# A transformer block in float32: the projections in another order, every input loaded in place

## The reference

```python
ctx_img = context[:, :257]; ctx_txt = context[:, 257:]
q = rms_norm(linear(layernorm(x), q_w, q_b), norm_q_w)          # 16 heads of 32
k = rms_norm(linear(ctx_txt, k_w, k_b), norm_k_w);  v = linear(ctx_txt, v_w, v_b)
k_img = rms_norm(linear(ctx_img, k_img_w, k_img_b), norm_k_img_w);  v_img = linear(ctx_img, v_img_w, v_img_b)
x = x + linear(attention(q, k_img, v_img) + attention(q, k, v), o_w, o_b)
# then a chain of small layers on the last token of each batch, a gate over all tokens, and a layer norm
```

## Time and profile before

| | |
|---|---|
| median of 3 runs | 604.54 us (603.22 to 607.73) |
| profiled execution | 605.41 us, its span 603.6 us |
| busy: PE, DVE, ACT, POOL | 533.3, 401.6, 282.0, 238.8 us |
| mean clock of TensorE granted | 0.952 of full speed |
| moved by DMA | 91.92 MB, mean 152 GB/s |

### The profile page before, as it was taken

How to read it: one execution, slowest core, us unless ns; L and a number is a source line. 1 busy time by engine, 2 the same in 40 slices (tenths; PEclk the granted TensorE clock), 3 DMA queues, 4 the chain that set the end, 5 groups by cost and what they waited for, 6 DMA issues and landing times.

```text
span 603.6 us, 9876 instructions
## 1 busy us (share of the span) xinstructions
PE 533.3 (88%) x3800; PEld 326.2 (54%) x3800; DVE 401.6 (67%) x783; ACT 282.0 (47%) x504; POOL 238.8 (40%) x138
## 2 busy tenths in 40 slices
PE   2599889999989999999999987899998999999860
PEld 2477667987655655555555553444353545454320
DVE  4547886522987788568875786566556666448676
ACT  2355844553135556436664342636252444376352
POOL 0033230022025677427655352152433063667453
PEclk9988989999989999989999987899899999799986
DMA  9506677499589778935987471707071623100001
GB/s 286 185 2 243 219 265 282 165 205 313 198 196 311 207 196 193 235 115 131 236 231 200 124 168 72 171 0 171 1 171 71 136 70 110 71 1 36 18 35 52
DMA packets 56512, 91.92 MB, mean 152 GB/s; under 512 B 5553, under 2 KB 30257, under 8 KB 55953
## 3 DMA queue, kind: packets, MB, share of 16 engines
q1 hardware_dynamic: 52000, 75.26, 45.5%
q0 software_dynamic: 3184, 14.16, 6.7%
q10 hardware_dynamic: 1280, 1.88, 1.0%
HBM read 71.08 MB, written 19.40 MB: 150 GB/s over the span
## 4 chain that ended last, share of the span: by engine, by line
PE 70%; DVE 15%; ACT 5%; POOL 4%; issue 2%; DMA 1%; ACTq 0%; POOLq 0%; DVEq 0%
PE psum L667 13%; PE psum L761 12%; PE psum L724 11%; PE psum L742 10%; PE psum L766 6%; PE psum L798 5%; DVE negt L1149 4%; PE psum L887 3%; PE psum L852 3%; PE psum L833 2%; DMA lows<-lows 1%; POOL ssum L1327 1%; POOL ssum L1325 1%; DVE qst L1179 1%; POOL ssum L1326 1%
## 5 line engine op out<-in xcount | busy, mean ns | idle before, releaser
L995 ACT ACTIVATE prob<-psum 128x512 f32<-128x512 f32 x256 | 138.7, 594 | 178.1 <-PE psum L742 178.0
L1149 DVE TENSOR_REDUCE negt<-psum 128x1 f32<-128x255 f32 (+1 forms) x256 | 129.2, 546 | 0.0
L1375 POOL TENSOR_TENSOR added<-added,prob 128x1024 f32<-128x1024 f32 x48 | 113.6, 2367 | 20.7 <-ACT prob L995 16.2
L724 PE MATMUL psum<-kst,qst 96*128 96x512 f32 x256 | 99.6, 466 | 4.9 <-DVE negt L1149 4.8
L1372 POOL TENSOR_TENSOR added<-prob 128x1024 f32<-128x1024 f32 x16 | 38.2, 2385 | 160.3 <-ACT prob L995 160.3
L742 PE MATMUL psum<-qst,kst 112*128 112x256 f32 x512 | 93.6, 303 | 1.9 <-ACT prob L995 1.8
L742 PEld LDWEIGHTS psum<-qst,kst 112*128 112x128 f32 x512 | 80.4, 197 | 24.8 <-ACT prob L995 10.9
L1147 DVE TENSOR_REDUCE negt<-psum 128x1 f32<-128x257 f32 x128 | 53.6, 419 | 60.3 <-PE psum L724 58.8
L761 PE MATMUL psum<-prob,vring 128*32 128x256 f32 x1152 | 91.9, 402 | 0.0
L724 PEld LDWEIGHTS psum<-kst,qst 96*128 96x128 f32 x256 | 41.2, 194 | 65.9 <-issue 40.3
L1325 POOL TENSOR_TENSOR ssum<-sq 128x512 f32<-128x512 f32 x6 | 9.6, 1598 | 110.8 <-ACT sq L960 110.8
(11 more groups left out here) (152 smaller groups left out, 678.0 us busy)
## 6 DMA issues: line engine op xcount, KB each, us to landing
kst<-kscr SPq DMA_DIRECT2D x96, 256.0 KB, 6.1
vring<-vscr SPq DMA_DIRECT2D x16, 576.0 KB, 8.4
kscr<-hl SPq DMA_DIRECT2D x16, 512.0 KB, 2.8
d<-d POOLq DMA_DIRECT2D x8, 1024.0 KB, 6.0
qst<-qscr SPq DMA_DIRECT2D x96, 64.0 KB, 6.2
vscr<-vbuf SPq DMA_DIRECT2D x18, 256.0 KB, 3.0
raw<-ctxT SPq DMA_DIRECT2D x4, 1024.0 KB, 5.1
qscr<-hl SPq DMA_DIRECT2D x8, 512.0 KB, 3.8
```

Of the source, the lines that this page charges most:

```text
L724: pe.matmul(psum[:, n % 3, :], qst[0:96, slot, jj, qt * P:(qt + 1) * P], kst[0:96, slot, jj, half * 512:(half + 1) * 512], start=True, sto ...
L995: act.activation(prob[:, r % NP, part], score2[:, part], ACT.Exp).then_inc(exp2_done, 1)
L1149: dve.tensor_reduce(negt[:, u % 2, qt, half, HPG + j:HPG + j + 1], psum[:, n % 3, k0:512], AX.X, ALU.max, negate=True)\
L1375: pool.tensor_tensor(added[:, :], added[:, :], prob[:, r % NP, :], ALU.add).then_inc(added_done, 1)
```

## The change

- **Order.** The second key tile of batch 0 comes first, then the first key tile, V of batch 0, xT and queries of half 1, xT and queries of half 0, keys (1,0), keys (1,1), V of batch 1. `TILE_TOKENS` says which of the two token buffers a tile reads.
- **First tile in pieces.** Its context tile and `wk` are loaded in four pieces each, split piece by piece, and PE runs `k01(kc)`: for each 128 input channels the three products of all four output chunks, in four banks.
- **In place.** `raw` is gone. Each input lands in the place of its own low part, which DVE then writes over it. All but one are issued at the start, without waits; `c11` is issued from ACT's queue (`late_ctx`) when tile 3 has been projected. `wk` and the four constants go on ACT's queue, the small late constants on SP's.
- **Loads apart.** `load_k` and `load_q` of units 0 and 1 have places of their own in the list.
- **Around V of batch 1.** S1(0) to S1(3) stand between the jobs of keys (1,1), S1(4) to S1(11) one to a job of V; the last four norms follow V jobs 4 to 7, and `shift(0)` job 4.
- POOL's memset of `chx` waits for the last sum of squares too.

```diff
+    split = lambda name: add('split', SPLIT_OF[name])
+    for kc in range(KC):
+        add('split', 2 * kc)
+        add('split', 2 * kc + 1)
+        add('k01', kc)
+    add('consts')
+    split('c00')
+    split('wki')
+    proj(0)
+    proj(1, (0,))
+    split('wvi')
+    proj(1, (1,))
+    split('wv')
+    proj(1, (2,))
+    add('sumsq', 0)
+    proj(1, (3,))
     add('xstat', 1)
     add('xnorm', 1)
+
+    for c in range(4):
+        v(0, (c,))
+        add('norm', 0, c)
+        if c == 1:
+            split('wq')
+        if c == 2:
+            add('sumsq', 1)
+    v(0, (4,))
+    add('xstat', 0)
+    add('norm', 1, 0)
+    v(0, (5,))
     for n in range(4):
         add('xT', 1, n)
+    add('norm', 1, 1)
+    v(0, (6,))
     add('xnorm', 0)
+    add('norm', 1, 2)
+    v(0, (7,))
+    add('norm', 1, 3)
+
+    proj(2, (0, 1, 2))
     for n in range(4):
         add('xT', 0, n)
+    proj(2, (3,))
+    add('load_k', 0)
+    split('c10')
+
+    proj(3, (0, 1))
+    add('sumsq', 2)
+    add('norm', 2, 0)
+    add('load_q', 0)
+    proj(3, (2,))
+    add('norm', 2, 1)
+    proj(3, (3,))
+    add('late_ctx')
+    add('norm', 2, 2)
+    add('norm', 2, 3)
+    add('load_k', 1)
+    add('load_q', 1)
+
+    proj(4, (0, 1))
+    add('sumsq', 3)
+    split('c11')
+    add('norm', 3, 0)
+    proj(4, (2,))
+    add('norm', 3, 1)
+    proj(4, (3,))
+    add('norm', 3, 2)
+    add('norm', 3, 3)
+
+    for oc in range(KC):
+        proj(5, (oc,))
+        if oc == 2:
+            add('sumsq', 4)
+        add('S1', oc)
+    after = {0: (('load_v', 0), ('load_v', 1), ('norm', 4, 0)), 1: (('norm', 4, 1),), 2: (('sumsq', 5), ('norm', 4, 2), ('norm', 4, 3)),
+             3: (('maxes', 0),), 4: (('norm', 5, 0), ('shift', 0)), 5: (('norm', 5, 1),),
+             6: (('norm', 5, 2),), 7: (('norm', 5, 3),)}
+    for c in range(CH):
         v(1, (c,))
+        add('S1', KC + c)
+        for e in after[c]:
+            add(*e)
     add('load', 2)
     add('phase2')
...
+TILES = [('k', 0, 1), ('k', 0, 0), ('q', 1), ('q', 0), ('k', 1, 0), ('k', 1, 1)]
+TILE_TOKENS = (0, 1, 1, 0, 1, 0)
+
+PIECES = [(n, kc) for kc in range(KC) for n in ('c01', 'wk')]
+SPLITS = [n for n, kc in PIECES] + ['c00', 'wki', 'wvi', 'wv', 'wq', 'c10', 'c11']
...
+            for kc in range(KC):
+                sp.dma_start(c_in['c01'][:, kc, :], ctx_of('c01')[:, kc, :]).then_inc(piece_loaded[2 * kc], 16)
+            load_c('c00')
+            load_w('wki')
+            load_w('wvi')
+            load_w('wv')
             load_x(1)
+            load_w('wq')
             load_x(0)
+            load_c('c10')
...
+            def load_q(u):
+                h, b, g = unit(u)
+                if u == 0:
+                    sp.wait_ge(lo_done, SPLIT_OF['c10'] + 1)
+                if u < 2:
+                    n = KC * TILES.index(('q', h)) + g
+                    for s in range(2):
+                        sp.wait_ge(hl_stored[s], 16 * ((n - s) // 2 + 1))
...
+            def k01(kc):
+
+                pe.wait_ge(lo_done, 2 * kc + 2)
+                for oc in range(KC):
+                    job = job_at[('proj', 0, oc, 0)]
+                    for a, b in ((0, 0), (0, 1), (1, 0)):
+                        mm = pe.matmul(psum[:, bank_of[job], :], w_parts['wk'][:, a, kc, oc * P:(oc + 1) * P],
+                                       token_parts[0][:, b, kc, :], start=(kc == 0 and a + b == 0), stop=(kc == KC - 1 and a == 1))
+                    if kc == KC - 1:
+                        mm.then_inc(job_done, 1)
...
+            for kc in range(KC):
+                act.dma_start(w_in['wk'][:, kc, :], T['wk'][kc * P:(kc + 1) * P, :]).then_inc(piece_loaded[2 * kc + 1], 16)
             for dst, src in ((ident[:, :], T['ident']), (colp[:], T['cols']), (ind_in[:, :], T['ind']), (lows[:, :], T['lows'])):
                 act.dma_start(dst, src).then_inc(const_loaded, 16)
 
-            def consts():
...
+            def late_ctx():
+                act.wait_ge(job_done, last_q[0] + 1)
+                act.dma_start(c_in['c11'][:], ctx_of('c11')).then_inc(in_loaded['c11'], 16)
```

More of the change, by code:

```diff
@@ L103, in make_plan @@
[L103 to L149, removed]
-        v(1, (c,))
[L151 to L160, removed]
@@ L268, in make_plan @@
     return plan
[L272 to L274 removed]
+TILES = [('k', 0, 1), ('k', 0, 0), ('q', 1), ('q', 0), ('k', 1, 0), ('k', 1, 1)]
+TILE_TOKENS = (0, 1, 1, 0, 1, 0)
+PIECES = [(n, kc) for kc in range(KC) for n in ('c01', 'wk')]
+SPLITS = [n for n, kc in PIECES] + ['c00', 'wki', 'wvi', 'wv', 'wq', 'c10', 'c11']
+SPLIT_OF = {n: i for i, n in enumerate(SPLITS)}
 JOBS = {'xT': 'dve', 'proj': 'act', 'sumsq': 'act', 'v': 'act', 'vimg': 'act', 'shift': 'dve', 'o': 'dve',
@@ L507, in last_job, with split_parts, ctx_of @@
             return max(n for n, e in enumerate(jobs) if test(e))
[L510 to L516, removed]
+        last_q = [last_job(lambda e: e[0] == 'proj' and e[1] == 3 - h) for h in range(2)]
+        def split_parts(i):
+            name = SPLITS[i]
+            if i < len(PIECES):
+                kc = PIECES[i][1]
+                if name == 'wk':
+                    return w_in['wk'][:, kc, :], w_parts['wk'][:, 0, kc, :], w_parts['wk'][:, 1, kc, :], piece_loaded[i]
+                return c_in['c01'][:, kc, :], token_parts[0][:, 0, kc, :], token_parts[0][:, 1, kc, :], piece_loaded[i]
+            if name[0] == 'w':
+                return w_in[name][:], w_parts[name][:, 0], w_parts[name][:, 1], in_loaded[name]
+            dst = token_parts[0 if name[2] == '1' else 1]
+            return c_in[name][:], dst[:, 0], dst[:, 1], in_loaded[name]
         last_k = last_job(lambda e: e[0] == 'proj')
+        def ctx_of(name):
+            c0 = int(name[1]) * KEYS + int(name[2]) * 512
+            return T['ctxT'].rearrange("(k p) n -> p k n", p=P)[:, :, c0:c0 + 512]
         block = ctx.enter_context(nc.Block())
@@ L593, in load @@
                         sp.dma_start(qst[row:row + 32, slot].bitcast(F32), src).then_inc(pair_loaded[slot], 16)
+            def load(u):
+                load_k(u)
+                load_q(u)
             def phase2():
@@ L631, in f_out @@
                   .then_inc(out_stored, 16)
-            steps = {'split': split, 'norm': norm, 'vstore': vstore, 'load': load, 'load_v': load_v, 'phase2': phase2,
+            steps = {'norm': norm, 'vstore': vstore, 'load_k': load_k, 'load_q': load_q, 'load': load, 'load_v': load_v, 'phase2': phase2,
                      'ch_row': ch_row, 'f_out': f_out}
@@ L928, in split @@
             def split(i):
[L929 to L934, removed]
+                src, hi, _, loaded = split_parts(i)
+                act.wait_ge(loaded, 16)
+                if SPLITS[i] == 'c10':
+                    act.wait_ge(job_done, last_q[1] + 1)
+                act.activation(hi, src, ACT.Copy).then_inc(hi_done, 1)
             def xstat(h):
```

105 lines of the change are left out of this document (46 added, 59 removed).

## The result

| | before | changed |
|---|---|---|
| median of 20 runs | 605.86 us (602.78 to 612.45) | 612.19 us (607.20 to 616.51) |
| profiled execution, its span | 605.41, 603.6 us | 613.36, 611.6 us |
| mean granted clock | 0.952 | 0.936 |

The ratio is 1.0098, with a 95% interval of 1.0075 to 1.0121. The change makes the kernel 1% slower. I had forecast 598, 1% faster.

The account below looks back on a forecast made before the run. PE has no gap from 200 us, so attention's start decides. S1(16) at 174.2 against 182.24 gains 8.0, less 1.3 for the clock: 6.7. 605.41 - 6.7 = 598.7, against the median 597.8, so 598; range 588 to 607.

Parts of the forecast that it names:

- Start and k01: First tile: eight ACT transfers issued by about 5.2 us, PE starts k01(0) at 8.3, its 48 matmuls end at 21.2.
- The constants: Wait before the second tile: constants land at 17 us, then DVE work until 22.6, a PE wait of 1.4.
- the third rival: Constants arrive late: ACT's queue slow, they land at 28 us, second tile at 32.6, 10 us lost, 608 us; chance 0.12.
- The dense stage: From the second tile PE runs dense through k(0,0), V, transposes and queries, ending at 78.2 us.
- T: The end of PE's dense stage, after q(1) and xT(0), forecast at 78.2 us.
- The stores that hold up DVE: After T: key loads delay query stores, DVE reduces S1(0) only after T + 40.6; PE waits 6.8 us, S1(3) ends at 129.4.
- The last norm and load(2): Around V of batch 1: norm(5,3) ends at 163.2, S1(16) follows 11.0 later at 174.2, PE waiting some 4 us.
- load(2) lands a first pair in about 8.2: Before S1(16): half a unit of issue, 4.1 us, and 4.6 for a transfer to land, less what overlaps.
- The restart: After the wait at S1(16) PE restarts at a low clock, worth 1.3 us of work.
- Everything after it is the same code in the same order: Premise of the sum: from S1(16), at 182.24 us before, nothing changes, so the gain there is kept.
- The rivals: Nobody is held up, 589 us (chance 0.22); the saving is handed back, 603 (0.18); constants arrive late, 608 (0.12).
- Handed back: Rival: before attention the store takes 10.1 us, POOL and DVE slow each other, 5 us later, 603 us; chance 0.18.

Follow-up runs that it names:

- a_pairs: The changed kernel with loads of units 2 and up again issued pair by pair, keys then queries of each pair: 595.93 us, ratio 0.9842 to the kernel before.
- a_late8: The changed kernel, keys first, with POOL's 1 MB weight loads two steps earlier in units 1 to 7 only: 603.21 us, ratio 0.9958 to the kernel before.

## Why the prediction was wrong, by its own steps

**Start and k01.** 8.3 forecast, 8.91 measured. The eight issues on ACT ended at 5.60 instead of 5.2. The 48 matmuls took 13.62 instead of 12.9 and ended at 22.53 instead of 21.2.

**The constants, and the third rival.** They were in at 15.95, DVE's first use of them, against my 17, and the second tile starts at 22.55 against 22.6, with no gap on PE (its first weight load waited 0.44). That the time fits is luck: the constants did not set it. DVE's subtraction for wki began at 20.20, behind ACT's copies, which waited for c00 until 15.78 and for wki until 18.25; by my rate those first 4 MB should have been in at 16.4. Had k01 ended at 21.2 as forecast, PE would have stood for 1.3 us, for wki and not for the constants. The rival that had ACT's queue starve until 28 is refuted: a megabyte of key pieces and the constants got through within 16 us. (That rival's second tile, 32.6, left out the 1 us of work on the constants: 33.6.) The Trainium skill (DMA: Bandwidth & Descriptors, Queues, rings and completion order) has each DMA engine take turns between its queues, from which the prediction made an estimate of 15. The measured 15.95 lies much nearer to it than to the 28 by ind_in's pace; but the prediction doesn't show how it came to 15, so this supports the rule only loosely.

**The dense stage.** T was to be 78.2; q(1)'s last job ends at 72.69 + 2.75 = 75.4. The mis-sized term is the transposes. I took the 3.2 us that 16 of them took before; by tile the changed kernel has

```profile
L705 PE MATMUL psum<-ident,xin x32: 270/272/273, 55.3 to 72.7; 128*128 128x128 f32 x32
```

and takes 1.7 for 16. Before they came after a gap, partly at half clock: the granted clock was 0.74 from 29 to 31 us and 0.50 from 31 to 33. Two times 1.5 us.

**The stores that hold up DVE.** DVE starts on S1(0) 42 us after T, at 117.34; the sum had 40.6. The wait for POOL was 1.77 (1.6) and for c11 1.57 (1.5). But the step gave PE's wait as one of 6.8 us for DVE. It was 3.03 for ACT at S1(0), whose second bank still held proj(5,0), then half clock (0.50 from 110 to 116), and 1.35 for DVE at S1(1). ACT in turn had waited for POOL to add up tile 4's squares:

```profile
107.65 1.59 POOL L1380 TENSOR_TENSOR ssum<-ssum,sq 128x512 f32<-128x512 f32 x1
...
109.27 0.69 ACT L1013 ACTIVATE raw<-psum,colp 128x512 f32<-128x512 f32 x1 [4.50 <-POOL ssum L1380]
```

The forecast has no such wait. So the time was nearly right and its split was not, which again is partly luck. S1(3) ends at 125.9 against 129.4, most of that from T.

**The last norm and load(2).** norm(5,3) was stored at 160.15 against 163.2. Up to here the forecast was 3 us too careful, about what T was off. (The 33.8 in it is also added up wrongly: eight tiles at 1.26, eight norms at 1.85, 1.8 and 6 make 32.7; it took 34.2.) Then it failed, in the term "load(2) lands a first pair in about 8.2". I had split a unit's issue into halves from a timeline in which pairs go in order, and hadn't read `load` in the diff for the order of its transfers. I had counted the transfers that stand ahead of others on SP's queue for units 0 and 1 only. Measured from the store to S1(16): 16.3 us instead of 11.0, a wait of 7.67 instead of 4. With the pairs in order it is 172.85 - 161.35 = 11.5 (a_pairs), so the term was right for the old order.

**The restart.** 1.3 us in the sum. From S1(16) to unit 0's end it took 10.3 before and 14.0 now, 3.7 more. In a_pairs it is 11.9, 1.6 more, near the forecast.

**"Everything after it is the same code in the same order".** This is the step that turned the sign. It was false: fourteen `load(u)` had changed. Unit 2 cost 8.7 us and unit 6 3.7 (from 294.46 to 315.56, against 17.4 before), small differences in the later units give 2.9 back. 5.8 - 3.7 - 8.7 - 3.7 + 2.9 = -7.4, which is what the last unit's end shows (560.96 against 553.58), and nearly all of the span's 8.0.

**The rivals.** None of the three is what happened. "Handed back" had the right direction and the wrong place. None looked beyond S1(16), since I had declared the rest unchanged.

## What to carry to other kernels

When a helper is split in two for the sake of one caller, look at the order that all its other callers get. In a queue that works in order, what counts is how much stands ahead of the first thing needed: issue the part that is consumed first, complete, before the part that is consumed second. And a stall on PE costs more than its length here, once as waiting and once as half clock behind it: 7.67 us cost another 3.7, 4.20 another 4.5, and the 5.85 of a_pairs another 1.6. So some spare time between a load's landing and its first use is worth more than it looks. Trace the first consumer of each load back to its issue before calling a stage unchanged.

## What the runs showed of the hardware that I had not expected

A 1 MB load from POOL's queue, issued at 167.21 in the kernel with all eight moved, inside a unit's load from SP, stretched the wait for that unit's queries from 7.67 to 15.51 us: the loads are on different queues and still delay each other. In a_late8, where that one load stays at 172.44, the wait is 7.67 again. And the half clock can stay for long: after the wait that ended at 219.30, with PE busy all the while, the granted clock was 0.50 until 226 and 0.61 over the next 4 us. In my sum such a restart was 1.3 us; here it was 3.7 to 4.5. It is not always so: after the 5.85 us of a_pairs the clock was 0.50 from 172 to 176 us and 0.92 over the next 4, and no run here shows what decides between the two.
